# The order of up and down products on TensorE in an expert layer: by single chunks in place of by twos

## The reference

```python
logits = xf @ Wg + bg
top_w, top_i = top_k(logits, 2)
top_w = softmax(top_w)
w_dense = sum(one_hot(top_i, E) * top_w[..., None], axis=1)
for e in range(E):
    h = gelu(xf @ W1[e] + b1[e])
    out = out + w_dense[:, e:e + 1] * (h @ W2[e] + b2[e])
```

## Time and profile before

| | before |
|---|---|
| runs | 2848.25, 2854.97, 2860.32 us |
| median | 2854.97 us |
| profiled execution | 2854.63 us |
| its span, first to last instruction | 2852.8 us |
| PE busy over the span | 2612.9 us |
| ACT busy over the span | 1555.2 us |
| DVE busy over the span | 1434.8 us |
| mean granted clock of PE | 0.943 |

### The profile page before, as it was taken

The page is one execution under the profiler, slowest core; times in us unless marked ns, Lnnn a source line. Parts: engine busy times, 40 slices in busy tenths (PEclk is TensorE's granted clock), DMA queues, the critical chain, the costliest instruction groups (busy, mean ns, idle before and its releaser), DMA issues. The chain is left out here.

```text
span 2852.8 us, 41228 instructions
## 1 busy us (share of the span) xinstructions
PE 2612.9 (92%) x12188; PEld 1131.4 (40%) x12188; DVE 1434.8 (50%) x2767; ACT 1555.2 (55%) x2248; POOL 357.1 (13%) x293
## 2 busy tenths in 40 slices
PE   8956787999999999999999999999799995699897
PEld 4422444333333333333333333333388884233222
DVE  6834777444444444444444444443387785234445
ACT  6620444555555555555555555555466663456555
POOL 3412332000000000000000000000266662000000
PEclk9978777999999999999999999999899997799898
DMA  5476444433233243343343332332011110222221
GB/s 166 142 151 143 113 122 115 96 77 88 64 83 87 59 88 80 67 88 73 73 88 67 80 88 59 88 82 65 9 39 36 39 39 30 55 61 81 59 71 65
DMA packets 117317, 226.60 MB, mean 79 GB/s; under 512 B 45218, under 2 KB 109570, under 8 KB 109954
## 3 DMA queue, kind: packets, MB, share of 16 engines
q1 hardware_dynamic: 117250, 225.79, 32.5%
HBM read 167.92 MB, written 57.80 MB: 79 GB/s over the span
## 5 line engine op out<-in xcount | busy, mean ns | idle before, releaser
L746 ACT ACTIVATE hidden<-hidden_psum,b 128x896 f32<-128x896 f32 x896 | 853.5, 1003 | 651.6 <-PE hidden_psum L694 651.6
L694 PE MATMUL hidden_psum<-tokens,w 64*128 64x448 f32 x3584 | 798.4, 564 | 9.9 <-DMA ident<-in_ident 7.1
L709 PE MATMUL y_psum<-hidden,w 128*64 128x448 f32 x3584 | 773.6, 553 | 2.1 <-DVE weighted L812 2.1
L812 DVE SCALAR_TENSOR_TENSOR weighted<-y_psum,b,w_bc 128x448 f32<-128x448 f32 x448 | 306.4, 684 | 868.4 <-PE y_psum L709 854.7
L694 PEld LDWEIGHTS hidden_psum<-tokens,w 64*128 64x128 f32 x3584 | 310.2, 187 | 472.9 <-ACT hidden L746 294.5
L709 PEld LDWEIGHTS y_psum<-hidden,w 128*64 128x64 f32 x3584 | 218.1, 136 | 502.5 <-issue 406.8
L188 ACT ACTIVATE ln_r<-ln_var,eps 128x448 f32<-128x448 f32 x280 | 177.4, 634 | 249.3 <-PE ln_var L173 126.5
L148 PE MATMUL ln_xc<-X,centre 128*128 (+1 forms) x448 | 236.2, 613 | 75.0 <-DVE X L574 55.5
L820 DVE TENSOR_TENSOR X<-X,weighted 128x448 f32 (+1 forms) x448 | 278.2, 621 | 2.9
L199 DVE SCALAR_TENSOR_TENSOR ln_q<-ln_var,ln_rr 128x448 f32<-128x448 f32 x280 | 173.4, 619 | 124.7 <-ACT ln_rr L194 123.3
L202 DVE SCALAR_TENSOR_TENSOR ln_g<-ln_q,ln_r 128x448 f32<-128x448 f32 x280 | 209.9, 749 | 9.6
(11 more groups left out here) (112 smaller groups left out, 1801.8 us busy)
## 6 DMA issues: line engine op xcount, KB each, us to landing
w_bc<-scr_wtok SPq DMA_DIRECT2D x112, 896.0 KB, 10.4
scr_xn<-xn SPq DMA_DIRECT2D x112, 224.0 KB, 1.9
tokens<-scr_xn SPq DMA_DIRECT2D x56, 224.0 KB, 2.6
tokens_plus_y<-scr_xn SPq DMA_DIRECT2D x56, 224.0 KB, 2.7
out<-out_tile SPq DMA_DIRECT2D x56, 224.0 KB, 1.9
X<-in_x SPq DMA_DIRECT2D x6, 1792.0 KB, 7.7
scr_xlr<-xn SPq DMA_DIRECT2D x112, 56.0 KB, 1.8
gated<-scr_xlr SPq DMA_DIRECT2D x8, 784.0 KB, 19.5
```

Of the source, the lines that this page charges most:

```text
L694: mm = pe.matmul(hp[:, s % 2, a, 0:TW], w1[rows_of, s * P:(s + 1) * P], S[rows_of, b, :], start=True, stop=True)
L709: mm = pe.matmul(yp[C * a:C * a + C, e % 2, 0:TW], w2[:, e, c, :], hs[:, s % (2 * CH0), a, :], start=(c == 0), stop=(c == CH0 - 1))
L746: act.activation(hs[:, k % (2 * CH0)], hp[:, k % 2, :, 0:TW], ACT.Gelu, bias=b1[:, e, c:c + 1])\
L812: dve.scalar_tensor_tensor(out=pr[:, e % 2], in0=yp[:, e % 2, 0:TW], scalar=b2[:, e:e + 1], in1=WB[:, b, e, :], op0=ALU.add, op1=ALU.mult) ...
```

## The change

The two functions `ups` and `downs` are replaced by one, `down`, that issues a single chunk. `body` now issues in step k the first chunk of up products of step k + 1, the first chunk of down products of step k, the second chunk of up products and the second chunk of down products. The waits of each chunk stay with it, and the transposes keep their place. No other engine's program is changed.

```diff
-                    def ups(u, b, e):
-                        for c in range(CH0):
-                            up(u, b, CH0 * e + c)
-
-                    def downs(u, b, e):
-                        for c in range(CH0):
-                            s = CH0 * e + c
-                            pe.wait_ge(gelu_done, SN * (2 * u + b) + s + 1)
-                            if c == 0:
-                                wait(pe, weighted, E * (2 * u + b) + e - 1)
-                            for a in range(2):
-                                mm = pe.matmul(yp[C * a:C * a + C, e % 2, 0:TW], w2[:, e, c, :], hs[:, s % (2 * CH0), a, :],
-                                               start=(c == 0), stop=(c == CH0 - 1))
-                            mm.then_inc(down_done, 1)
+                    def down(u, b, e, c):
+
+                        s = CH0 * e + c
+                        pe.wait_ge(gelu_done, SN * (2 * u + b) + s + 1)
+                        if c == 0:
+                            wait(pe, weighted, E * (2 * u + b) + e - 1)
+                        for a in range(2):
+                            mm = pe.matmul(yp[C * a:C * a + C, e % 2, 0:TW], w2[:, e, c, :], hs[:, s % (2 * CH0), a, :],
+                                           start=(c == 0), stop=(c == CH0 - 1))
+                        mm.then_inc(down_done, 1)
 
                     def body(u, top2, move, last):
...
                         for k in range(2 * E):
                             if k == 1 and move:
                                 transpose(u + 1)
-                            if k + 1 < 2 * E:
-                                ups(u, (k + 1) // E, (k + 1) % E)
-                            elif not last:
-                                ups(u + 1, 0, 0)
-                            downs(u, k // E, k % E)
-
-                    ups(0, 0, 0)
+                            for c in range(CH0):
+                                if k + 1 < 2 * E:
+                                    up(u, (k + 1) // E, CH0 * ((k + 1) % E) + c)
+                                elif not last:
+                                    up(u + 1, 0, c)
+                                down(u, k // E, k % E, c)
+
+                    for c in range(CH0):
+                        up(0, 0, c)
                     transpose(0)
                     every_unit(pe, body)
```

## The result

| | before | after |
|---|---|---|
| runs, us | 2848.25 to 2860.32 (4) | 3005.64 to 3014.54 (4) |
| median, us | 2855.84 | 3010.61 |
| profiled execution, us | 2854.63 | 3005.64 |
| span, us | 2852.8 | 3003.8 |

The ratio after to before is 1.0544, with a 95% interval of 1.0513 to 1.0575: the kernel is 155 us slower at the medians, 5.4%. The medians include the runs taken beside the changed kernel.

What follows compares the result with a forecast made beforehand. PE was taken to bound layer 0's experts, busy throughout. 447 steps at about 0.35 us for added shape switches make 156 us; with profiled execution 2854.63 that is 3010.6, or 3011 at the median, range 2997 to 3026.

Steps and rivals of the forecast that it cites:

- PE bounds the stage: Layer 0's experts, 522 to 2021 us: PE busy 1499.00 of 1499.00 us, so its own order sets the time.
- The price of a switch: PE changing array shape between up and down products: 0.355 us there and back; 0.35 x 447 steps = 156 us added.
- The two parts of the price: At each switch: first pair starts later (0.095 and 0.10 us), then second pair waits for its weight load (0.055 and 0.105).
- Waits of the moved chunks: PE's waits for gelus and y banks in the new order: 1.6 and 2.5 us to spare for gelus, no cost.
- SP's queue: SP's loads of next tokens and weights: a whole tile, 27 us or more, for transfers of 10.4 us; no cost.
- Loads hidden: Rival, chance 0.05: weights ready at each switch, only the later start of 0.195 us a step added, 87 us, 2942.
- The clock falls: Rival, chance 0.04: more PE gaps drop the granted clock to 1.2 GHz in part of the stage; 3160 us.
- The gap is a wait: Rival, chance 0.03: PE's gap at a switch is a wait for ACT's gelu; 2855 us, or 159 us less.
- The gelus were to wait about 800 us: Layer 0's gelus on ACT should still wait for PE alone, about 800 us instead of 651.6.
- the waits at the stage's start: In the first steps PE also waits for other engines; some 2 us of the added time may disappear there.

Runs made afterwards that it cites:

- narrow load: The changed kernel with up products that load 72 columns of weights in place of 128: 2964.0 us, ratio to before 1.0396.
- one-shape kernel: Up products issued in the down products' array shape, in the changed kernel's order (2698.7 us) and in the order before (2700.2 us).

## Why the prediction was right

It said 3011 us, and 3010.6 was measured. That these agree to half a microsecond is luck: the runs lie 9 us apart, and the profiled execution, forecast at 3010.6, took 3005.64, since the code behind the stage took 7.5 us less. What was right is the price and where it falls. Point by point:

- *PE bounds the stage, before and after.* Right: 1653.00 of 1653.00 us busy in the window after; its products waited for another engine only at the stage's start.
- *The price of a switch.* Right in size: 0.35 us a step was the value taken, 3.710 - 3.359 = 0.351 was found, and 447 x 0.351 = 156.9 us. The 0.355 of the single rows was 0.004 too much, since a pair takes 0.376 us and not 0.375. Layer 1's pattern in the earlier trace rows, which the same trace held, gave the new groups to the hundredth. The stage's end moved by 158.6 us, 157.1 once its later beginning is taken off (500.05 after, 498.58 before, the first up group in each timeline).
- *The two parts of the price.* The later start and the uncovered load were read from two consecutive starts. The narrow load shows the load's part: 41.1 us of the stage for 56 columns less at 894 switches, 0.046 us each, the 0.046 that was worked out from 0.105 us for 128 columns. What makes the later start itself was not taken apart: the runs show only that it goes with the change of shape.
- *Waits of the moved chunks at nothing.* Right: the idle time ahead of L694 and L705 stayed at 9.5 and 1.8 us. SP's queue cost nothing either.
- *Loads hidden* (0.05) would have given 2942. The timeline of the changed kernel has no load ahead of a switch. The Trainium skill (TensorE: Matmul & The Clock Gate, Step-by-step: what each phase is for) has loads pulled ahead of matmuls in flight; the trace agrees inside one shape, where they start under the running pair (1004.63 and 1005.00 in the one-shape kernel), and not across a change of shape. There the rule of the Trainium skill's TensorEngine Tiling (Array Packing), Key Properties, that a change of mode drains the engine, fits the traces, where the next load and pair start 0.47 us after the last pair; that a drain is what holds them was not shown.
- *The clock falls* (0.04): it did not; 1.00 throughout the window.
- *The gap is a wait* (0.03): refuted by the one-shape kernels, which keep the waits and lose the gap.

One detail was off. The gelus were to wait about 800 us, and waited 759.4. Their busy time rose by 49.9 us (853.5 to 903.4) for the same 896 gelus, and that and the 107.8 us of added waiting make 157.7. Before, two gelus ran back to back in 1.91 us, less than two alone (a single one is 1.0); after, each stands alone, and what two neighbours had shared is counted as busy. And of the waits at the stage's start that might have hidden 2 us of the cost, 0.3 us went (2.1 to 1.8 ahead of the down products).

## What to carry to other kernels

When PE bounds a stage and its matmuls come in two array shapes, count the changes of shape and price one from starts in the timeline; the busy share hides it, since the gap is counted as busy. Group products of one shape as far as the PSUM buffers let the next engine keep up, and after regrouping set the places of the once-a-unit work, transposes and small cross-engine steps, anew: here unsuited places ate some 72 of 79 us. If a switch is named as a wait for some engine, see whether the length stays when the name changes, as it did with the 0.70 us ahead of the up groups.

## What had not been expected of the hardware

Different operands, PSUM banks and accumulation cost nothing between neighbouring products of one shape: up and down products in turn started 0.376 us apart, the same as within a kind, and 2698.7 and 2700.2 us for the two orders are equal within their runs. I had expected at least a trace of a pause where PE turns to another PSUM bank and another operand.
